# Graph layers on one core: value splits moved from VectorE to ScalarE and GpSimd in the first row tiles, the first z matmul ahead of layer 2's weights, input loads ahead of the adjacency

## The reference

```python
def _L0(x, inp, adj, w):                       # masked dot-product attention
    anchor_adj = einsum('md,de,ne->mn', x, w, inp)
    scores = where(adj > 0, anchor_adj, -2**32 + 1)
    atten = softmax(scores / 0.07, axis=1)
    return atten @ inp
def _L1(x, adj, W, a1, a2):                    # graph attention
    Wh = x @ W
    e = leaky_relu((Wh @ a1)[:, None] + (Wh @ a2)[None, :], 0.2)
    att = softmax(where(adj > 0, e, -9e15), axis=1)
    return elu(att @ Wh)
x = layernorm(x + _L0(x, L0_gnn_input, adj, L0_gnn_weight))
x = layernorm(x + _L1(x, adj, L1_gnn_W, L1_gnn_a1, L1_gnn_a2))
```

## Time and profile before

| | |
|---|---|
| median of 3 runs | 1493.58 us |
| the profiled execution | 1494.69 us |
| its span | 1492.9 us |
| TensorE matmul busy | 1439.6 us (96%) |
| VectorE busy | 1326.4 us (89%) |
| ScalarE busy | 1065.3 us (71%) |
| GpSimd busy | 982.8 us (66%) |
| mean granted TensorE clock | 0.989 |

### The profile page before, as it was taken

How to read it: one execution, slowest core, us unless ns; L and a number is a source line. 1 busy time by engine, 2 the same in 40 slices (tenths; PEclk the granted TensorE clock), 3 DMA queues, 4 the chain that set the end, 5 groups by cost and what they waited for, 6 DMA issues and landing times.

```text
span 1492.9 us, 28265 instructions
## 1 busy us (share of the span) xinstructions
PE 1439.6 (96%) x9853; PEld 1030.7 (69%) x9853; DVE 1326.4 (89%) x2303; ACT 1065.3 (71%) x2327; POOL 982.8 (66%) x629
## 2 busy tenths in 40 slices
PE   7799999999999999999999999987999999999996
PEld 4477777777777777777777777774566666666664
DVE  5999999999999999999999999967779797979794
ACT  4588888888888888888888888877745454546463
POOL 6455555555555555555555555527999999999995
PEclk9999999999999999999999999998999999999998
DMA  7889889888898889899989888753334343444420
GB/s 253 241 236 257 232 241 257 246 241 235 250 260 238 238 243 254 240 238 251 255 235 244 245 256 231 195 114 86 85 64 100 84 99 84 98 86 94 90 57 14
DMA packets 378766, 278.81 MB, mean 187 GB/s; under 512 B 307713, under 2 KB 354049, under 8 KB 378625
## 3 DMA queue, kind: packets, MB, share of 16 engines
q1 hardware_dynamic: 378624, 277.01, 70.3%
HBM read 160.56 MB, written 40.89 MB: 135 GB/s over the span
## 4 chain that ended last, share of the span: by engine, by line
PE 90%; POOL 3%; DVE 2%; issue 2%; ACT 1%; DMA 1%; SPq 0%; ACTq 0%; POOLq 0%; DVEq 0%
PE ps L541 16%; PE ps L563 13%; PE ps L623 11%; PE ps L616 10%; PE ps L543 8%; PE ps L574 8%; PE ps L576 8%; PE ps L575 8%; PE ps L600 5%; POOL p_lo L460 2%; PE ps L634 1%; DMA inp_sb<-inp 1%; ACT rows L730 1%; POOL vals_lo L456 1%; DVE rows L866 1%
## 5 line engine op out<-in xcount | busy, mean ns | idle before, releaser
L404 POOL TENSOR_SCALAR edges<-neg_mask 128x1536 uint8<-128x1536 bf16 x192 | 285.0, 1484 | 329.3 <-DVE neg_mask L841 329.0
L730 ACT ACTIVATE rows<-rows,exp_bias 128x512 f32<-128x512 f32 x576 | 415.2, 721 | 40.5 <-DVE exp_bias L933 40.5
L460 POOL TENSOR_TENSOR p_lo<-p,p_hi 128x1024 fp32r<-128x1024 f32 x180 | 426.5, 2408 | 13.2 <-PE ps L600 7.7
L960 DVE SCALAR_TENSOR_TENSOR p<-ps,e_col,edgesT 128x1024 f32<-128x1024 f32 x288 | 349.0, 1277 | 62.2 <-PE ps L593 37.5
L866 DVE CUSTOM_DVE_ANT_0 rows<-ps,neg_mask 128x1024 f32<-128x1024 f32 x288 | 351.1, 1219 | 32.3 <-PE ps L576 26.0
L717 ACT CAST pT_hi<-ps 128x512 f16<-128x512 f32 x432 | 252.1, 583 | 135.7 <-PE ps L563 127.7
L541 PE MATMUL ps<-vals,pT_hi 128*128 128x256 f16 x1728 | 331.8, 273 | 1.2 <-ACT att L710 0.8
L759 ACT CAST p_hi<-p 128x1024 fp32r<-128x1024 f32 x180 | 185.1, 1047 | 176.6 <-DVE p L960 174.4
L543 PE MATMUL ps<-vals,pT_lo 128*128 128x128 f16 x1728 | 308.6, 219 | 0.0
L875 DVE TENSOR_TENSOR pT_lo<-ps,pT_hi 128x512 f16<-128x512 f32 x432 | 287.8, 684 | 17.3 <-ACT pT_hi L717 17.3
L563 PE MATMUL ps<-ident,rows 128*128 128x128 f32 x1728 | 263.6, 275 | 7.4 <-DVE pT_lo L875 6.4
(11 more groups left out here) (108 smaller groups left out, 1731.0 us busy)
## 6 DMA issues: line engine op xcount, KB each, us to landing
adj_sb<-adj SPq DMA_DIRECT2D x192, 768.0 KB, 5.3
edge_rows<-edges SPq DMA_DIRECT2D x192, 192.0 KB, 4.8
xq<-x SPq DMA_DIRECT2D x48, 64.0 KB, 2.6
xr<-x SPq DMA_DIRECT2D x48, 64.0 KB, 1.9
out<-y_w SPq DMA_DIRECT2D x5, 512.0 KB, 3.7
inp_sb<-inp SPq DMA_DIRECT2D x3, 768.0 KB, 10.1
inp_sb<-inp_sb SPq DMA_TRANSPOSE x96, 5.1
edgesT<-edge_rows SPq DMA_TRANSPOSE x48, 5.6
```

Of the source, the lines that this page charges most:

```text
L460: nc.gpsimd.tensor_tensor(p1_lo[:, m % LO_SLOTS, :], p1[:, (NB * g + n) % P_SLOTS, :], p1_hi[:, m % HI_SLOTS, :].bitcast(F32), ALU.subtrac ...
L730: nc.scalar.activation(row_chunk(1 - par, c), row_chunk(1 - par, c), ACT.Exp, bias=exp_bias[:, 1 - par:2 - par], scale=EXP_SCALE, accum_ou ...
L960: nc.vector.scalar_tensor_tensor(out=p1[:, (NB * g + n) % P_SLOTS, :], in0=ps[:, R_ROW:R_ROW + 2, :].rearrange("p b w -> p (b w)"), scalar ...
```

## The change

Four things are changed, all of them before or within the first two row tiles.

1. SyncE's loads: w0 first and on a semaphore of its own, then the input's first piece, x, the input's second and third pieces, and only then the first quarter of adj; the two last pieces of the input alternate with quarters of adj. w1, a1 and a2 come behind adj's third quarter.
2. TensorE turns w0 alone, then the input and x, and makes the first z. w1 is turned at c = 1 of tile 1 and its products are made at c = 4; VectorE takes them out at c = 6 (`weight_sums`). `attend` waits for that, since they share a PSUM bank.
3. The high halves of `vals` are made by ScalarE, one instruction per chunk at each step of tile 0 (`vals_high`).
4. The low halves are made by GpSimd, two instructions per chunk: one scales `inp_sb` in place by 64, the other subtracts the high half (`vals_low`). They wait until the chunk was turned and its high half made. They stand between the edges of tiles 0 and 1.

```diff
+            sp.dma_start(w0_sb, w0).then_inc(w0_in, 16)
+            load_inp(0)
+            sp.dma_start(xq[:], pair_rows(x, 0)).then_inc(xq_in, 16)
+            load_inp(1)
+            load_inp(2)
+            load_first_adj(0)
+            load_inp(3)
+            load_first_adj(1)
+            load_inp(4)
+            load_first_adj(2)
             sp.dma_start(w1_sb[:], w1).then_inc(weights_in, 16)
             sp.dma_start(a21[:, 1:2], a1.rearrange("(d a) -> d a", a=1)).then_inc(weights_in, 16)
             sp.dma_start(a21[:, 0:1], a2.rearrange("(d a) -> d a", a=1)).then_inc(weights_in, 16)
...
+            load_first_adj(3)
@@ gpsimd
-            for i in range(len(INP_CHUNKS)):
-                pool.wait_ge(inp_in[i], 16)
-                nc.gpsimd.tensor_scalar(vals[:, inp_blocks(i), 0:P], inp_sb[:, inp_blocks(i), :], SPLIT_SCALE, None,
-                                        ALU.mult).then_inc(vals_hi, 1)
+            def vals_low(c):
+                b = slice(c * BPC, (c + 1) * BPC)
+                pool.wait_ge(inp_turned, c + 1)
+                pool.wait_ge(vals_hi, c + 1)
+                nc.gpsimd.tensor_scalar(inp_sb[:, b, :], inp_sb[:, b, :], SPLIT_SCALE, 0.0, ALU.mult,
+                                        ALU.add).then_inc(vals_scaled, 1)
+                pool.wait_ge(vals_scaled, c + 1)
+                nc.gpsimd.tensor_tensor(vals[:, b, P:2 * P], inp_sb[:, b, :], vals[:, b, 0:P],
+                                        ALU.subtract).then_inc(vals_lo, 1)
@@ tensor
+            turn_inp(0)
             turn_x(0, 0)
-            turn_inp(0)
-            pe.wait_ge(wa_copied, 1)
+            pe.wait_ge(w0_copied, 1)
+            make_z(0)
+            turn_inp(1)
+            turn_inp(2)
             pe.wait_ge(xT_lo_set, 1)
-            for c in range(Z_LEAD):
-                turn_inp(c + 1)
-                make_z(c)
+            make_z(1)
...
+                    if known == 1 and c == 1:
+                        turn_w1()
+                    if known == 1 and c == 4:
+                        make_wa()
@@ scalar
+            def vals_high(c):
+                b = slice(c * BPC, (c + 1) * BPC)
+                act.wait_ge(inp_in[piece_of(c)], 16)
+                nc.scalar.activation(vals[:, b, 0:P], inp_sb[:, b, :], ACT.Copy, scale=SPLIT_SCALE).then_inc(vals_hi, 1)
...
+                        vals_high(c)
@@ vector
-                    if t == 0 and c >= 5 and c % 2 == 1:
-                        vals_low((c - 5) // 2)
-                    if t == 1 and c < 8:
-                        vals_low(c + 4)
+                    if t == 1 and c == 6:
+                        weight_sums()
```

More of the change, by code:

```diff
@@ L308, in _, with load_inp, load_first_adj @@
             inp_rows = inp.rearrange("(b p) d -> p b d", p=P)
-            sp.dma_start(w0_sb, w0).then_inc(weights_in, 16)
+            def load_inp(i):
+                blocks = inp_blocks(i)
+                sp.dma_start(inp_sb[:, blocks, :], inp_rows[:, blocks, :]).then_inc(inp_in[i], 16)
+            def load_first_adj(q):
+                sp.dma_start(adj_sb[:, q, :], pair_rows(adj, 0)[:, q * QW:(q + 1) * QW]).then_inc(adj_in[q], 16)
+            sp.dma_start(w0_sb, w0).then_inc(w0_in, 16)
[8 more added lines that the diff above has]
+            load_first_adj(2)
             sp.dma_start(w1_sb[:], w1).then_inc(weights_in, 16)
@@ L405, in make_edges @@
                                         ALU.add).then_inc(edges_set, 1)
-            for q in range(QUARTERS // 2):
-                make_edges(0, q)
+            vals_low(0)
+            vals_low(1)
+            make_edges(0, 0)
+            vals_low(2)
+            vals_low(3)
+            make_edges(0, 1)
+            for c in range(4, 7):
+                vals_low(c)
             def score_cols(j):
@@ L443, in tile_rstd @@
                     make_edges(t + 1, 0)
+                    if t == 0:
+                        vals_low(9)
                     make_edges(t + 1, 1)
+                if t == 0:
+                    vals_low(10)
+                    vals_low(11)
                 if ends_tile(known):
@@ L486, in _, with turn_w1, make_wa @@
             pe.wait_ge(ident_set, 1)
-            pe.wait_ge(weights_in, 64)
-            nc.tensor.transpose(ps[:, MISC, 0:P], w0_sb, ident[:])
-            nc.tensor.transpose(ps[:, MISC, P:2 * P], w1_sb[:], ident[:]).then_inc(wT_turned, 1)
-            pe.wait_ge(wT_copied, 1)
-            for k in range(2):
-                nc.tensor.matmul(ps[:, PV, k * P:(k + 1) * P], a21[:, k:k + 1].to_broadcast([P, P]), w1T, start=True, stop=True)
-            pe.wait_ge(avg_set, 2)
-            nc.tensor.matmul(ps[:, PV, 2 * P:3 * P], averager[:], w1_sb[:], start=True, stop=True).then_inc(wa_made, 1)
+            pe.wait_ge(w0_in, 16)
+            nc.tensor.transpose(ps[:, PV, 0:P], w0_sb, ident[:]).then_inc(w0_turned, 1)
+            def turn_w1():
+                pe.wait_ge(weights_in, 48)
+                nc.tensor.transpose(ps[:, PV, 3 * P:4 * P], w1_sb[:], ident[:]).then_inc(wT_turned, 1)
+            def make_wa():
+                pe.wait_ge(wT_copied, 1)
+                for k in range(2):
+                    nc.tensor.matmul(ps[:, PV, k * P:(k + 1) * P], a21[:, k:k + 1].to_broadcast([P, P]), w1T, start=True,
+                                     stop=True)
+                pe.wait_ge(avg_set, 2)
+                nc.tensor.matmul(ps[:, PV, 2 * P:3 * P], averager[:], w1_sb[:], start=True, stop=True).then_inc(wa_made, 1)
             def turn_x(t, par):
@@ L669, in _ @@
         def _(act):
-            act.wait_ge(wT_turned, 1)
-            nc.scalar.copy(w0T, ps[:, MISC, 0:P])
-            nc.scalar.copy(w1T, ps[:, MISC, P:2 * P]).then_inc(wT_copied, 1)
+            act.wait_ge(w0_turned, 1)
+            nc.scalar.copy(w0T, ps[:, PV, 0:P]).then_inc(w0_copied, 1)
             def inpT_out(c):
@@ L685, in xT_high @@
                 nc.scalar.activation(xT_hi[:, par, :], ps[:, MISC, 0:P], ACT.Copy, scale=SPLIT_SCALE).then_inc(xT_hi_set, 1)
+            inpT_out(0)
             xT_high(0, 0)
-            inpT_out(0)
-            for c in range(Z_LEAD):
-                inpT_out(c + 1)
-                z_high(c)
+            z_high(0)
+            inpT_out(1)
+            inpT_out(2)
+            z_high(1)
             def score_sums(j):
@@ L705, in tile_steps @@
                             z_high(c + Z_LEAD)
+                        vals_high(c)
+                    if known == 1 and c == 2:
+                        act.wait_ge(wT_turned, 1)
+                        nc.scalar.copy(w1T, ps[:, PV, 3 * P:4 * P]).then_inc(wT_copied, 1)
                     if c == ATT_STEP and ends_tile(known):
```

26 lines of the change are left out of this document (10 added, 16 removed).

## The result

The changed kernel takes **1483.36 us** (median of 6 runs, 1483.2 to 1484.52) against 1493.77 (6 runs, 1492.31 to 1494.64) for the kernel before beside it. The ratio is 0.9932, interval 0.9919 to 0.9945. 10.4 us are gained where 13.0 were forecast. The profiled execution took 1483.2 us with a span of 1481.4, TensorE 97% busy, clock 0.993.

A forecast was written before the change was run, and what follows sets the result against it. VectorE was taken to bound the kernel from about 20 to 67 us, after TensorE's wait for input; 5.2 + 11.5 - 0.7 (weight sums) - 2.0 - 1.0 = 13.0 us gained, so 1480.6 us, range 1476.5 to 1489.0.

The forecast's parts named there:

- Loads: At the start: the input's third piece lands at 9.6 us, so TensorE's chunks start 5.2 us earlier.
- First mask: On VectorE at the start: it waits for adj until 12.0 us and delays later `z_low`; term -2.0 us.
- Low halves off VectorE: Tiles 0 and 1: VectorE loses its twelve low halves of `vals`, gaining 11.5 us.
- The lock: Tiles 0 and 1: masks wait for GpSimd instructions they meet, 5.1 us for ten against 4.2 before; term -1.0 us.
- The rival of starved masks: VectorE's masks can't get between GpSimd's back-to-back instructions, waiting for three each: slower, 1507.5 us; chance 0.05.
- ScalarE: Tile 0: twelve extra copies at 0.60 us, 1.8 us per chunk within TensorE's 1.97; no cost.
- GpSimd's scaling: Low halves on GpSimd: 0.6 us per scaling; at 1.5 us GpSimd binds, a rival at 1489.0 us, chance 0.22.
- GpSimd stays hidden by 2.6 us: Up to tile 2: GpSimd allows tile 1's bias down to 53.3 us, below the forecast 55.9, so VectorE decides.
- TensorE is full from there on: After tile 1's bias TensorE has no gaps, 19.9 us per tile, so the bias's whole advance shortens the launch.
- M: End of tile 0's `moved_low` on GpSimd, about 54 us; its transpose lands 6.2 later, first used 6.9 after tile 1's bias.
- G: Experiments' explanation of tile 2's lost 3.3 us: GpSimd's lateness reaches TensorE through the transposes, so ScalarE waits for a DMA.
- V: Experiments' explanation of tile 2's lost 3.3 us: GpSimd's lateness reaches TensorE through VectorE, whose masks wait for GpSimd instructions.

The follow-up runs named there:

- f: Changed kernel with the low halves of `vals` back on VectorE, one instruction per chunk; high halves stay on ScalarE: 1487.68 us.
- b: Kernel before with only the values moved to ScalarE and GpSimd, its loads and weights' start kept: 1486.84 us.
- d: Changed kernel with GpSimd's scaling in the one-operation form (multiply alone) instead of multiply and add 0: 1492.99 us.
- h: Changed kernel with two buffers each for `moved_hi` and `moved_lo`, so ScalarE's cast needn't wait for tile 0's transposes; no instruction moved: 1483.12 us.
- c: Changed kernel with tile 0's `moved_low` and DMA transposes two edges sooner, all instructions kept: 1483.29 us.
- j: Changed kernel with the same instructions, GpSimd's reordered and held at six places until VectorE's next mask is done: 1482.12 us.
- e: Changed kernel without GpSimd's scaling; `vals` holds the input itself instead of 64 times it, GpSimd only subtracts: 1481.91 us.
- i: Changed kernel with e and j together: no scaling, GpSimd's instructions reordered and held for masks: 1480.12 us.
- l: k, with GpSimd's second `moved_low` also held until VectorE has made tile 3's first mask: 1479.92 us.
- k: i, with the bias of tile 0 ahead of the last mask of that tile on VectorE: 1479.90 us.

## Why the prediction was right, and where it was wrong

**The verdict and the range held; the mechanism held up to the end of tile 1.** X, the bias of tile 1, came at 54.8 where 55.9 was forecast. By its terms:

- *Loads.* The third piece was issued at 2.67 and landed 6.9 us later, at the 9.6 that were forecast. But its first chunk was turned at 10.66 (before: 14.83), so 4.2 us were won and not 5.2. TensorE had no wait left on a DMA there; it came from z(0), turns 1 and 2 and z(1), with ScalarE's copies between them. Its instructions were slower there than later, too: a pair of z matmuls took 2.05 us at 6.06 and 1.02 at 11.10. The forecast hadn't looked at this chain, and why they were slower is not shown.
- *First mask.* Forecast for 12.0, it came at 12.10, but not because of adj, whose first quarter was issued at 3.30 and landed 8.2 us later, at 11.5: it started right behind VectorE's second `z_low`. The term of -2.0 isn't in the rows: from 10.66 on TensorE took a chunk each 1.94 us without a wait, and VectorE still idled 2.7 us for z between 14 and 23 us.
- *Low halves off VectorE.* None is in its groups. f puts this at 4.3 to 4.7 us net of all that it costs on GpSimd, so the 11.5 us in the sum were gross; b's 6.4 us hold both moves.
- *The lock.* Mean mask 1.26 us in tiles 0 and 1 (forecast 1.45): 3.1 us over free ones where 5.1 was forecast and 4.2 was before. This term was +1.1 us, not -1.0. The rival of starved masks fell: none of the ten took more than 1.93 us. With 4.2 + 11.5 - 0.7 - 2.0 + 1.1 the sum is 14.1, and 14.2 was measured. That they agree so well is partly luck: the -2.0 isn't borne out, and one wait is not in the sum: VectorE stood 1.28 us for a quarter of adj at 39.4, since SyncE issues that load behind a store that waits for GpSimd's edges, and these now stand behind low halves.
- *ScalarE.* The copies took 0.62 us. Only GpSimd's first low half waited for one, the first, and TensorE for none.
- *GpSimd's scaling.* The first took 0.62 us, as taken from L404. L397's 1.51 was the other end, and d shows that it is real: it goes with the form of one operation. The choice "by the form" was right. Why the form decides no run shows. The mean of twelve was 0.83, since four of them (1.20 to 1.33 us) met masks.

**The step that failed** is "GpSimd stays hidden by 2.6 us", and with it "TensorE is full from there on". The prediction's own inequality shows it: M + 6.2 should lie below X + 6.9. M was 57.54 instead of 54, X 54.78 instead of 55.9, so 63.7 stands against 61.7, 2.0 us on the wrong side. M's 3.5 us are no single item. The first low half began 1.35 us late. The eight edges took 15.0 us and not 11.8, and the scalings 10.0 and not 7.2: together 6.0 us for locks, where 5 was set down. The subtractions took 0.7 more. So M took 3.5 us and X, by coming early, 1.1 of a margin of 2.6.

And the inequality looked at the wrong reader. It took TensorE's first use of a moved chunk as the deadline; that wait was 0.37 us. What waited before it was ScalarE, whose cast overwrites `moved_hi` and so needs the transpose done 4.70 us sooner than it was, and VectorE, whose mask met `moved_low` itself. h took away the first and c the first at the price of the second, and neither gained; j took the first away too, left the mask behind `moved_low` in tile 1 as c did, kept the masks of tile 2 nearly free (0.95 to 1.12 us), and gained about 1 us without any less work; e took the backlog away and got tile 2 back to 20.0, though from a later start. So most of the 3.3 us are GpSimd's backlog, through two paths that hide one another. G alone is refuted by c and h. V alone is not shown either: its times came out in c and h, but in c its masks waited elsewhere than it said, and in b its time was 3.3 us off. In c, h and i, where ScalarE's cast waits no longer, a mask of tile 2 meets the second `moved_low`, and TensorE waits 1.54, 1.58 and 1.21 us for VectorE behind it. In the changed kernel, in e and in j no mask of tile 2 was held behind that `moved_low`.

That the forecast was near is in part the sum of errors that cancel: X came 1.1 us sooner than forecast, and 3.3 us were lost where nothing was expected to be.

The Trainium skill's "SBUF — State Buffer", section "Who interferes with whom", also says that a VectorE instruction with two SBUF inputs contends with a GpSimd instruction that reads; by that rule the trace of l agrees: L965 took 1.35 us beside the edges, and the next one of the same form and size, L969, which began at 71.55 when the edges had ended (71.38), 0.35.

**Open.** TensorE's idle time in tile 2 of the changed kernel is 2.4 us of the 3.3. The other 0.9 stand in its busy time, 20.91 us for 173 matmuls where e has 20.00 for 173; this wasn't traced further. In i, k and l tile 2 keeps 1.1 to 1.5 us over 20.0, of which 1.2 in i and k is TensorE's wait for VectorE behind the mask that met the second `moved_low`. l took this wait away and tile 2 kept 1.1, for which its trace names no single cause. e's later bias of tile 0 is argued only. The bias of tile 0 lies up to 1.0 us apart among kernels that are alike up to it (34.98 in the changed kernel, 35.95 in h), so differences of single biases below 1 us tell nothing. The prediction had no term for TensorE's clock. Before, from 30 to 67 us, the granted clock was 0.86 on average; VectorE was busy for 34.9 of these 37 us, so what a faster TensorE could have given there is at most the 2.1 us that it idled. No run isolates it.
